# Convolution by interpolated products with two mixing stages: another order of the preparation, and attention maps with a pixel's blocks side by side

## The chip, the cores and the metric

The kernel runs on one core of a Trainium2 chip, as one program with one launch. The metric is the device time in microseconds of one execution. TensorE (PE) multiplies matrices into PSUM, ScalarE (ACT) and VectorE (DVE) read PSUM and work elementwise, GpSimd (POOL) does small things, and SyncE (SP) issues nearly all DMAs. Each engine takes its own instructions in order; they wait for each other through semaphores.

## The reference

The input is x, [4, 256, 48, 48] in float32. One layer is computed:

```
x = x + conv_attention(layer_norm_over_channels(x))
t = tokens(x);  t = t + ffn(layer_norm(t));  x = back(t)

conv_attention(x):
    k = relu(conv7x7(x, w1, dilation 2, padding 6) + b1)         # 256 -> 128 channels
    k = relu(batch_norm(w2 k + b2));  attn = softmax(k, 49 taps)
    out = sum over the 49 taps p of  x shifted by p  *  attn[:, p]
ffn: router on the mean token, two of 8 experts (256 -> 512 -> 256, gelu), weighted sum, layer norm
```

## The kernel before, in words

**Images.** With dilation 2, each of the four input images falls apart into four independent images of 24 x 24 pixels by the parity of row and column. These are the 16 images (`IMGS`) n = 0 to 15, four (`BI`) to each of the batches b = 0 to 3. A row strip `t` is 4 rows, 96 pixels, and an image has NT = 6 strips.

**Convolution.** Each row of the 7-tap kernel is done by evaluation at 14 points k (`NP`). The taps are transformed into `U`, the images into `V`, each split into a high and a low float16 part. Then `conv(b, k, c)` makes 21 matmuls (7 tap rows, three products of high and low parts) for channel half c, into one of three banks of `pM`. ScalarE (`copy_m`) and VectorE (`y_points`, L1009 to L1020) combine them into the 128 channels.

**Preparation.** Before the first product, `U` and the first four images of `V` must be there. The work is in four pairs of weight groups (`PAIRS_OG`), each pair with seven steps j (`U_PAIR`). `turn_u(u)`, u = 7 pair + j, is eight matmuls of a piece of weights with the table `Gs` (L1326). `turn_v(m)` is six matmuls with the table `Td` (L1311), and an image has six of them (`V_TURNS`). In the kernel before, `turn_v` m = 6 pair + j - 1 follows `turn_u` in the steps j = 1 to 6 of its pair: image n is turned in pair n. ScalarE writes the high halves (`u_high` L796, `v_high` L792), VectorE the low halves (`u_low` L965, `v_low` L961). TensorE may begin `turn_u(u)` when `u_low(u - 2)` is done, and `turn_v(m)` when `v_low(m - 2)` is done.

Between these, in the same in-order queues: for each pair, ScalarE sums the magnitudes of both weight groups (`magnitude(g)`, L784), VectorE puts them on a diagonal (`spread_mags`, L972), TensorE multiplies that (`bound`, L1333), VectorE makes the scale and the table `Gs` out of it (`tap_scale`, L979 to L995, whose last write is `back_w`), and the pair's first `turn_u` waits for that. For each image, VectorE takes the statistics (`ln_stats` L943, `ln` L952 to L956), GpSimd the inverse root (`rsqrt`, L719 to L725), ScalarE normalises in place (`normalise_x` L775) and writes the high half (`x_high` L840), VectorE the low half (`x_low` L1076), and `turn_v` waits for that. The order is written out by hand with constants that say in which step j each of them comes (`MAGS_THEN`, `NORM_PARTS`, `LN_PARTS`, `XHI_AT`, `SPREAD_AT`, `V_LATE`). On SyncE's queue the order of loads is: `ident`, weights 0 and 1, image 0, two tables, image 1, `w2` and small parameters, image 2, weights 2 to 5.

**Attention maps.** After a batch's logits and softmax, `turn_a(b, i)` (L1397) transposes the 49 taps of an image strip by strip into two banks, three strips of 96 pixels each. `a_high` (L833) and `a_low` (L1071) copy them as two float16 parts into a map of 49 rows and `MAP` = 600 columns: 576 pixels and 24 columns of padding. For batches 0 to 2 one instruction on each engine takes both banks. The maps of images 0 to 7 are stored to DRAM by DMA and loaded back in the last batch, those of 8 to 11 are written where they are read.

**Spreading.** An image is also cut into NB = 5 blocks of 5 rows (`TB` = 120 pixels; the last has 4 rows). `spread_taps(u)` (L1428) makes, for one pixel place in all blocks of all images of its group, one matmul whose moving operand is one column per image and block, out of the map `aT[g]`. In the map before, the blocks of a pixel lie `TB` columns apart. An item is 8 such matmuls (group 0: images 0 to 11, 60 or 48 columns) or 24 (group 1: images 12 to 15, 20 or 16 columns). Items go round three banks: item u waits until the low half of item u - 3 is taken (`spread_high` L869 on ScalarE, `spread_low` L1149 on VectorE). The 33 early items of group 0 are placed behind the convolution's halves of the last batch by `EARLY_SLOTS`: four behind (k = 9, c = 1), four behind each half at k 10 and 11, four and three at k 12, three and three at k 13. VectorE has `y_points` between the items of k 11 and of k 12 and searches maxima of expert weights (`take_unit`) up to k 10. After the last, `attend(n)` (L1444) multiplies the spread taps with the images, ScalarE evicts (`evict` L857), and the feed-forward part follows.

## Time and profile before

| | us |
|---|---|
| median of 3 runs | 963.73 (961.29 to 965.79) |
| the profiled execution, device time | 960.01 |
| its span, first to last instruction | 958.2 |
| TensorE busy | 904.5 (94%) |
| VectorE busy | 694.6 (72%) |
| ScalarE busy | 529.1 (55%) |
| GpSimd busy | 139.9 (15%) |
| mean granted TensorE clock | 0.975 |

The profile gives, for each engine, busy time and instruction counts, then the span in 40 slices, the chain of work that ended last, and groups of instructions with their mean duration and what ended the idle time before them.
### The profile page before, as it was taken

How to read it: one execution, taken by the hardware profiler on the slowest of the kernel's cores; microseconds unless marked ns; L12 is line 12 of the kernel's file. 1: busy time of each engine (PE TensorE's matmuls, PEld its weight loads, DVE VectorE, ACT ScalarE, POOL GpSimd, SP SyncE). 2: the span in 40 equal slices, each digit the busy share in tenths (PEclk: the TensorE clock that was granted, in tenths of full speed). 3: DMA queues.
4: the chain of work that ended last, by engine and by line, in shares of the span. 5: the costliest groups of instructions: out<-in, count | busy, mean ns of one | idle time of the engine just before them, and what ended most of it. 6: DMA issues, size and time to landing. Idle time of an engine off the chain costs nothing. (4 is left out here: it accounts for less than half of the span.)

```text
span 958.2 us, 19556 instructions
## 1 busy us (share of the span) xinstructions
PE 904.5 (94%) x7679; PEld 754.2 (79%) x7679; DVE 694.6 (72%) x1798; ACT 529.1 (55%) x981; POOL 139.9 (15%) x163
## 2 busy tenths in 40 slices
PE   2788999999999999999999959999999999999997
PEld 2777788888888888888999946777777777777776
DVE  3787467577658547865779858778877887788767
ACT  4796443543354321234445638768786878687751
POOL 1100100100001010200123211211212121212122
PEclk9799999999999999989999969999999999999999
DMA  9631132123210144540567563642465246323211
GB/s 222 185 95 50 50 80 70 52 57 98 58 34 26 41 137 143 175 79 2 149 181 216 149 176 78 153 104 53 98 151 101 50 100 165 84 69 82 67 34 50
DMA packets 134826, 95.01 MB, mean 99 GB/s; under 512 B 63579, under 2 KB 129516, under 8 KB 134636
## 3 DMA queue, kind: packets, MB, share of 16 engines
q1 hardware_dynamic: 134734, 93.77, 39.0%
q8 instruction: 60, 0.98, 0.4%
q14 instruction: 32, 0.26, 0.1%
HBM read 54.91 MB, written 29.40 MB: 88 GB/s over the span
## 5 line engine op out<-in xcount | busy, mean ns | idle before, releaser
L1340 PE MATMUL pM<-V,U 128*128 128x264 f16 (+3 forms) x2352 | 289.2, 280 | 2.2 <-DVE V L961 2.2
L1340 PEld LDWEIGHTS pM<-V,U 128*128 128x128 f16 x2352 | 227.8, 98 | 44.2 <-DVE U L965 2.4
L1876 ACT ACTIVATE gf<-pH,b1c,sc 128x384 f32<-128x384 f32 x192 | 127.6, 668 | 81.8 <-issue 67.2
L2166 PE MATMUL pH<-V,w1h 128*128 128x384 f16 x768 | 157.7, 328 | 1.8 <-ACT w1h L1848 1.8
L2180 PE MATMUL pY<-w2h,gh 128*128 128x256 f16 x576 | 157.0, 273 | 0.9 <-DVE w2l L2027 0.9
L2180 PE MATMUL pY<-w2l,gh 128*128 128x256 f16 x576 | 157.0, 273 | 0.0
L2180 PE MATMUL pY<-w2h,gl 128*128 128x256 f16 x576 | 157.0, 273 | 0.0
L2035 DVE SCALAR_TENSOR_TENSOR gl<-gf,sc,gh 128x384 f16<-128x384 f32 x192 | 112.0, 620 | 47.9 <-ACT gh L1867 47.9
L1867 ACT ACTIVATE gh<-gf,sc 128x384 f16<-128x384 f32 x192 | 115.4, 616 | 0.0
L2166 PEld LDWEIGHTS pH<-V,w1h 128*128 128x128 f16 x768 | 75.5, 98 | 50.0 <-issue 3.4
L792 ACT CAST V<-pV 128x336 f16<-128x336 f32 x96 | 41.8, 437 | 113.0 <-PE pV L1311 113.0
L2166 PE MATMUL pH<-V,w1l 128*128 128x384 f16 x384 | 94.5, 328 | 0.0
L961 DVE TENSOR_TENSOR V<-pV,V 128x336 f16<-128x336 f32 x96 | 47.1, 500 | 60.2 <-ACT V L792 60.2
L1815 POOL TENSOR_TENSOR tb<-V,bet 128x768 f32<-128x768 f32 x24 | 43.7, 1819 | 301.7 <-DVE z L2047 279.1
L1311 PE MATMUL pV<-Td,xs 96*128 96x168 f16 x576 | 58.4, 238 | 7.1 <-DVE xs L1076 6.2
L2180 PEld LDWEIGHTS pY<-w2h,gh 128*128 128x128 f16 x576 | 56.4, 98 | 8.9 <-issue 1.2
L2180 PEld LDWEIGHTS pY<-w2l,gh 128*128 128x128 f16 x576 | 56.4, 98 | 7.7
L775 ACT ACTIVATE xa<-xa,shift,rstd 96x256 f32<-96x256 f32 x96 | 49.7, 592 | 22.9 <-POOL shift L721 22.9
L2180 PEld LDWEIGHTS pY<-w2h,gl 128*128 128x128 f16 x576 | 56.4, 98 | 6.5
L719 POOL TENSOR_TENSOR rstd<-ve,mhalf 96x6 f32<-96x6 f32 x16 | 21.1, 1320 | 274.0 <-DVE nmean L956 274.0
L2166 PEld LDWEIGHTS pH<-V,w1l 128*128 128x128 f16 x384 | 37.6, 98 | 25.5 <-DVE w1l L1997 0.6
L1311 PEld LDWEIGHTS pV<-Td,xs 96*128 96x128 f16 x576 | 46.6, 99 | 12.1 <-issue 5.8
(251 smaller groups left out, 1351.9 us busy)
## 6 DMA issues: line engine op xcount, KB each, us to landing
xa<-in_xt SPq DMA_DIRECT2D x16, 576.0 KB, 6.5
xs_scratch<-xs SPq DMA_DIRECT2D x16, 576.0 KB, 4.3
V<-t_scratch SPq DMA_DIRECT2D x24, 384.0 KB, 3.7
out<-o SPq DMA_DIRECT2D x23, 384.0 KB, 2.9
xs<-in_ew SPq DMA_DIRECT2D x16, 512.0 KB, 4.3
U<-xs_scratch SPq DMA_DIRECT2D x16, 480.0 KB, 4.7
V<-in_w1g SPq DMA_DIRECT2D x6, 784.0 KB, 8.4
w1r<-in_ew SPq DMA_DIRECT2D x8, 512.0 KB, 4.4
```

The lines of the kernel that those rows point to most:

```text
L719: nc.gpsimd.tensor_tensor(rstd[:, n % 2], ve[:, n % 2], mhalf[:, :], ALU.pow).then_inc(rstd_step, 1)
L775: last = nc.scalar.activation(xa[:, n % XBUFS, t, :], xa[:, n % XBUFS, t, :], ACT.Identity, bias=shift[:, n % 2, t:t + 1], scale=rstd[:, n ...
L792: nc.scalar.copy(v_out(0, m), v_in(m)).then_inc(vhi_ready, 1)
L961: tt(v_out(1, m), v_in(m), v_out(0, m), ALU.subtract).then_inc(vlo_ready, 1)
L1311: last = nc.tensor.matmul(v_in(m)[:, :, r * TR * TILES:(r + 1) * TR * TILES], xs[:, n % 2, 2 * g + r, a, c * P:(c + 1) * P], Td[:, d, :], ...
L1340: return nc.tensor.matmul(out[:, :, first:end], U[:, k, hi_u, piece, :], V[:, b % 2, hi_v, k, c, :, first + TILES * d:end + TILES * d], st ...
L1815: nc.gpsimd.tensor_tensor(tb[:, s], tk[:, m % TBUFS], bet[:, None, :].broadcast_to([P, CT, C]), ALU.add).then_inc(bias_added, 1)
L1867: nc.scalar.activation(gh[:, s, j, :], gf[:, (JB * m + j) % GBUFS, :], ACT.Copy, scale=scale_of(G_UP)).then_inc(gh_ready, 1)
L1876: nc.scalar.activation(gf[:, (JB * m + j) % GBUFS, :], pH[:, (JB * n + j) % HBUFS, 0:CN], ACT.Gelu, bias=b1c[:, j // FB, j % FB:j % FB + 1 ...
L2035: stt(gl[:, sl, j, :], gf[:, (JB * m + j) % GBUFS, :], scale_of(G_UP), gh[:, sl, j, :], ALU.mult, ALU.subtract).then_inc(g_step, 1)
L2166: last = nc.tensor.matmul(pH[:, (JB * n + j) % HBUFS, 0:CN], w[:, k, c, f * P:(f + 1) * P], xT[:, s, x, c, :], start=(i == 0), stop=(i == ...
L2180: last = nc.tensor.matmul(pY[:, t, 0:C], g[:, s, j, t * P:(t + 1) * P], w[:, j // FB, j % FB, :], start=(i == 0), stop=(i == len(terms) - 1))
```

## The change

Part one changes the order of the preparation. `turn_v`, with its high and low halves, follows three steps behind the weights for images 0 to 2 (`V_LEAD` = 3: m = u - 3 for u = 3 to 20); image 3 stays in the steps j = 1 to 6 of pair 3. Weights 2 are loaded before image 1 and weights 3 after it. ScalarE takes the magnitude of group 2 before the loop and half of that of group 1; VectorE sums the other half (`add_half`). ScalarE does `u_high(0)` first, then normalises image 0, then `u_high(1)` and `x_high(0)`. The constants become pairs, one for pair 0 and one for the later pairs. In the later pairs `bound`, `spread_mags` and `tap_scale` come one step earlier than before. GpSimd's root for the batch norm comes after image 1's instead of image 2's.

Part two changes the maps of the first three batches: column `place * NB + block` instead of `block * TB + place`. The map is written in two pieces, strips 0 to 4 (480 columns, the four whole blocks) from the first bank and strip 5 (96 columns) from the second. `spread_taps` reads contiguous runs of `nb` columns for group 0. Group 1 is unchanged.

```diff
-    MAGS_THEN = (1, 3)
-    V_LATE = U_PAIR - V_TURNS
+    MAGS_THEN = ({3: 1}, {0: 0, 2: 1})
+    V_LEAD, V_LATE = 3, U_PAIR - V_TURNS
-    LN_PARTS, NORM_PARTS = {1: 0, 2: 1, 3: 2}, {0: 0, 2: 1, 4: 2}
-    XHI_AT, SPREAD_AT, BN_AT, LN_BACK_AT = 5, 4, 4, 5
+    LN_PARTS, NORM_PARTS = ({4: 0, 5: 1, 6: 2}, {1: 0, 2: 1, 3: 2}), ({4: (0, 1), 5: (2,)}, {1: (0,), 3: (1,), 4: (2,)})
+    XHI_AT, SPREAD_AT, BOUND_AT, SCALE_AT = (6, 5), (4, 3), (5, 4), (6, 5)
+    BN_AT, LN_BACK_AT = 5, 5
...
+        def turn_at(pair, j):
+
+            u = U_PAIR * pair + j
+            if pair < PAIRS_OG - 1:
+                return range(max(0, u - V_LEAD), max(0, u - V_LEAD + 1))
+            return range(V_TURNS * pair + j - V_LATE, V_TURNS * pair + j - V_LATE + 1) if j >= V_LATE else range(0)
...
+        def map_rows(flat, h):
+
+            rows = flat.rearrange("p (r w t) -> p t r w", r=BROWS, t=NB)
+            return rows[:, 0:NB - 1] if h == 0 else rows[:, NB - 1, 0:TL // SIDE]
+
+        def map_strips(n, h):
+
+            if n < EARLY:
+                return (range(NT - 1), range(NT - 1, NT))[h]
+            return range(h * NT // 2, (h + 1) * NT // 2)
...
+            load_w(sp, 2)
             load_x(1)
+            load_w(sp, 3)
...
-            for g in range(2, W_HOMES):
+            for g in range(4, W_HOMES):
                 load_w(sp, g)
...
-                    nc.gpsimd.memset(aTs[:, :, :, PIX:MAP], 0.0).then_inc(map_pads, 1)
+                    nc.gpsimd.memset(aTs[:, :, :, MAP - SIDE * NB + NB - 1:MAP:NB], 0.0).then_inc(map_pads, 1)
...
+                rows = KS * C // OG // (2 if g == 1 else 1)
...
-                parts, found = map_parts(b, i)
-                for h, (part, bank) in enumerate(found):
-                    act.wait_ge(aT_ready, 2 * n + (h + 1) * 2 // parts)
-                    nc.scalar.copy(map_to(n, 0, part, parts), bank).then_inc(ahi_ready, 2 // parts)
+                for h in range(2):
+                    act.wait_ge(aT_ready, 2 * n + h + 1)
+                    nc.scalar.copy(map_to(n, 0, h), map_from(n, h)).then_inc(ahi_ready, 1)
...
-            for g in range(2):
+            for g in range(3):
                 magnitude(g)
-            normalise_x(0)
...
-                    if pair + j == 0:
-                        x_high(0)
-                    if j >= V_LATE:
-                        v_high(V_TURNS * pair + j - V_LATE)
...
+                    if pair == 0 and j < 2:
+                        (x_high if j else normalise_x)(0)
+                    for m in turn_at(pair, j):
+                        v_high(m)
...
+            def add_half():
+                here, rest = mags[:, 1:2], mags[:, OGS:OGS + 1]
+                dve.wait_ge(w_loaded[1], 16)
+                nc.vector.tensor_reduce(rest, wst[1][:, KS * C // 2:], AX.X, ALU.add,
+                                        apply_absolute_value=True).then_inc(mag_added, 1)
+                dve.wait_ge(mag_added, 1)
+                dve.wait_ge(mag_ready, 2)
+                tt(here, here, rest, ALU.add).then_inc(mag_added, 1)
+                dve.wait_ge(mag_added, 2)
...
-                    first = block_0 * TB + h * SIDE + w % MO * TILES + w // MO
+                    place = h * SIDE + w % MO * TILES + w // MO
+                    where = (slice(place * NB + block_0, place * NB + block_0 + nb) if g == 0 else
+                             slice(block_0 * TB + place, (block_0 + nb - 1) * TB + place + 1, TB))
                     last = nc.tensor.matmul(spread_banks[u % SBANKS][:, o:o + imgs * nb], G[0:LO + TAPS, v, at:at + P],
-                                            aT[g][0:LO + TAPS, :, first:first + (nb - 1) * TB + 1:TB], start=True, stop=True)
+                                            aT[g][0:LO + TAPS, :, where], start=True, stop=True)
```

## Rows read from the trace of the kernel before

**Rows 1.** Stretches: us from:to, length, busy us (instructions) per engine, clock, DMA, GB/s.
```profile
0.00:20.00 20.00, 6.04 (x15) 4.97 (x16) 7.46 (x39) 5.94 (x8) 2.46 (x12) 1.00 0.97 216
...
140.00:300.00 160.00, 159.14 (x1523) 139.00 (x1522) 110.36 (x311) 69.91 (x137) 14.88 (x32) 1.00 0.23 60
...
422.91:430.55 7.64, 7.64 (x55) 6.41 (x54) 6.10 (x14) 2.23 (x4) 0.10 (x1) 0.73 0.00 0
```

**Rows 2.** Timeline, TensorE, preparation: start, us, instructions, [idle before <-releaser].
```profile
15.05 3.35 PE L1326 MATMUL pM<-work,V 112*128 112x224 f32 x8 [1.66 <-DVE back_w L995]
...
26.07 1.00 PE L1311 MATMUL pV<-Td,xs 96*128 96x168 f16 x6 [5.22 <-DVE xs L1076]
26.86 3.26 PE L1326 MATMUL pM<-work,V 112*128 112x224 f32 x8
...
43.20 2.54 PE L1326 MATMUL pA<-work,V 112*128 112x224 f32 x8 [2.08 <-DVE back_w L995]
...
96.31 9.83 PE L1340 MATMUL pM<-V,U 128*128 128x288 f16 x84 [2.19 <-DVE V L961]
```

**Rows 3.** Timeline, ScalarE, head of the preparation.
```profile
18.92 3.06 ACT L775 ACTIVATE xa<-xa,shift,rstd 96x256 f32<-96x256 f32 x6 [7.08 <-POOL shift L721]
...
22.67 1.47 ACT L840 CAST xs<-xa 96x1536 f16<-96x1536 f32 x1
...
27.44 1.70 ACT L784 ACTIVATE U<-V 112x1792 f32<-112x1792 f32 x1
```

**Rows 4.** Timeline, VectorE, head of the preparation.
```profile
17.03 2.05 DVE L943 BATCH_NORM_STATS2 st<-xa 96x6 f32<-96x256 f32 x6
...
22.80 1.09 DVE L965 TENSOR_TENSOR U<-pM,U 128x896 f16<-128x896 f32 x1 [2.90 <-ACT U L796]
```

**Rows 5.** DMA issues from 4.15 to 4.6 us: size, us from issue to landing (image 1).
```profile
xa<-in_xt SPq DMA_DIRECT2D x1, 576.0 KB, 11.7
```

**Rows 6.** One line's instructions: count, ns min/median/max, first to last start, form.
```profile
L833 ACT CAST xa<-pA x4: 632/632/632, 384.0 to 401.1; 49x576 f16<-49x576 f32 x4
...
L1071 DVE TENSOR_TENSOR xa<-pA,xa x4: 751/752/752, 384.8 to 401.9; 49x576 f16<-49x576 f32 x4
```

**Rows 7.** Timeline, TensorE, last batch and the stage after it.
```profile
400.34 0.66 PE L1397 MATMUL pA<-ident,E 96*66 96x96 f32 x6 [0.92 <-DVE xa L1071]
...
422.02 1.07 PE L1428 MATMUL pV<-xa,U 113*128 113x60 f16 x8
422.91 4.26 PE L1340 MATMUL pM<-V,U 128*128 128x288 f16 x21
...
427.88 1.07 PE L1428 MATMUL pL<-xa,U 113*128 113x60 f16 x8
428.77 1.97 PE L1428 MATMUL pV<-xa,U 113*128 113x60 f16 x16
430.55 3.86 PE L1340 MATMUL pM<-V,U 128*128 128x288 f16 x21
...
441.11 0.87 PE L1428 MATMUL pL<-xa,U 113*128 113x48 f16 x8
441.80 2.60 PE L1340 MATMUL pM<-V,U 128*128 128x288 f16 x21
...
452.14 0.51 PE L1444 MATMUL pM<-U,V 120*120 120x256 f16 x3 [1.21 <-issue]
...
513.51 0.90 PE L1428 MATMUL pL<-U 113*128 113x16 f16 x24
514.25 2.07 PE L1428 MATMUL pV<-U 113*128 113x20 f16 x48
```

**Rows 8.** Timeline, ScalarE, last batch.
```profile
421.34 0.56 ACT L869 CAST V<-pV 120x480 f16<-120x480 f32 x1 [0.33 <-PE pV L1428]
```

**Rows 9.** Timeline, VectorE, last batch.
```profile
421.93 0.66 DVE L1149 TENSOR_TENSOR V<-pV,V 120x480 f16<-120x480 f32 x1 [0.23 <-ACT V L869]
...
424.66 1.62 DVE L1015 SCALAR_TENSOR_TENSOR work<-pM,work 128x288 f32<-128x288 f32 x4
```

More of the change, by code:

```diff
@@ L547, in map_of, with map_to, map_from @@
             return aT[g][hl * LO:hl * LO + TAPS, n - GROUPS[g][0], :]
-        def map_parts(b, i):
-            if b < B - 1:
-                return 1, [(slice(0, PIX), pA[0:TAPS, :, 0:PIX // 2])]
-            return 2, [(slice(h * PIX // 2, (h + 1) * PIX // 2), a_bank(b, i, h)[0:TAPS, 0:PIX // 2]) for h in range(2)]
-        def map_to(n, hl, part, parts):
-            to = map_of(n, hl)[:, part]
-            return to.rearrange("p (h x) -> p h x", h=2) if parts == 1 else to
+        def map_rows(flat, h):
[5 more added lines that the diff above has]
+            return range(h * NT // 2, (h + 1) * NT // 2)
+        def map_to(n, hl, h):
+            if n < EARLY:
+                return map_rows(map_of(n, hl), h)
+            return map_of(n, hl)[:, h * PIX // 2:(h + 1) * PIX // 2]
+        def map_from(n, h):
+            bank = a_bank(n // BI, n % BI, h)[0:TAPS, 0:len(map_strips(n, h)) * TT]
+            if n < EARLY and h == 0:
+                return bank.rearrange("p (t r w) -> p t r w", t=NB - 1, w=SIDE)
+            return bank.rearrange("p (r w) -> p r w", w=SIDE) if n < EARLY else bank
         def sizes_of(b, numbers):
@@ L728, in _ @@
             rsqrt(1)
-            rsqrt(2)
             pool.wait_ge(bn_step, 1)
-            pool.wait_ge(size_step, 6)
+            pool.wait_ge(size_step, 4)
             nc.gpsimd.tensor_tensor(bnp[:, 6:7], bnp[:, 5:6], mhalf[0:TAPS, 0:1], ALU.pow).then_inc(bn_rstd, 1)
-            for n in range(3, IMGS):
+            for n in range(2, IMGS):
                 rsqrt(n)
@@ L783, in magnitude @@
                     act.wait_ge(mag_ready, g)
[L784 removed]
+                rows = KS * C // OG // (2 if g == 1 else 1)
+                nc.scalar.activation(spots[0:OG * KS, 0:rows, :], wst[g].rearrange("p (r n) -> p r n", n=OG)[:, 0:rows], ACT.Abs,
                                      accum_out=mags[:, g:g + 1]).then_inc(mag_ready, 1)
@@ L970, in spread_mags @@
                 for a in range(2):
+                    if pair == 0 and a == 1:
+                        add_half()
                     dve.wait_ge(mag_ready, 2 * pair + a + 1)
@@ L1067, in a_low @@
                 n = BI * b + i
-                parts, found = map_parts(b, i)
-                for h, (part, bank) in enumerate(found):
-                    dve.wait_ge(ahi_ready, 2 * n + (h + 1) * 2 // parts)
-                    tt(map_to(n, 1, part, parts), bank, map_to(n, 0, part, parts),
-                       ALU.subtract).then_inc(alo_ready, 2 // parts)
+                for h in range(2):
+                    dve.wait_ge(ahi_ready, 2 * n + h + 1)
+                    tt(map_to(n, 1, h), map_from(n, h), map_to(n, 0, h), ALU.subtract).then_inc(alo_ready, 1)
             def x_low(n):
@@ L1186, in _ @@
             for pair in range(PAIRS_OG):
+                late = min(pair, 1)
                 for j in range(U_PAIR):
-                    if j == U_PAIR - 1 and pair + 1 < PAIRS_OG:
+                    if j == SCALE_AT[late] and pair + 1 < PAIRS_OG:
                         tap_scale(pair + 1)
                     u_low(U_PAIR * pair + j)
-                    if pair + j == 0:
+                    if pair == 0 and j == 1:
                         x_low(0)
-                    if j >= V_LATE:
-                        v_low(V_TURNS * pair + j - V_LATE)
-                    if j in LN_PARTS and pair + 2 < BI:
-                        if LN_PARTS[j] < 2:
-                            ln_stats(pair + 2, third(LN_PARTS[j]))
+                    for m in turn_at(pair, j):
+                        v_low(m)
+                    if j in LN_PARTS[late] and pair + 2 < BI:
+                        if LN_PARTS[late][j] < 2:
+                            ln_stats(pair + 2, third(LN_PARTS[late][j]))
                         else:
                             ln(pair + 2, third(2))
-                    if j == SPREAD_AT and pair + 1 < PAIRS_OG:
+                    if j == SPREAD_AT[late] and pair + 1 < PAIRS_OG:
                         spread_mags(pair + 1)
@@ L1394, in turn_a @@
                 for h in range(2):
-                    for t in range(NT // 2):
-                        at = (h * NT // 2 + t) * TAPS
-                        last = nc.tensor.transpose(a_bank(b, i, h)[0:EPAD, t * TT:(t + 1) * TT],
+                    for slot, t in enumerate(map_strips(n, h)):
+                        at = t * TAPS
+                        last = nc.tensor.transpose(a_bank(b, i, h)[0:EPAD, slot * TT:(slot + 1) * TT],
                                                    E[:, i, at:at + EPAD], ident[0:TT, 0:TT])
@@ L1405, in _ @@
                     turn_u(U_PAIR * pair + j)
-                    if pair == 0 and j == V_LATE:
+                    if pair == 0 and j == V_LEAD:
                         pe.wait_ge(tab_loaded, 16)
-                    if j >= V_LATE:
-                        turn_v(V_TURNS * pair + j - V_LATE)
-                    if j == U_PAIR - 2 and pair + 1 < PAIRS_OG:
+                    for m in turn_at(pair, j):
+                        turn_v(m)
+                    if j == BOUND_AT[min(pair, 1)] and pair + 1 < PAIRS_OG:
                         bound(pair + 1)
```

16 lines of the change are left out of this document (9 added, 7 removed).

## The prediction

> **What bounds the kernel now.** I read three views in order: busy time by stretch, the timelines of TensorE, ScalarE and VectorE in the stages that the diff touches, and the waits there. The first [rows 1] says which resource matters: in the middle of the convolution (140 to 300 us) TensorE is busy 159.14 of 160 us, so work of other engines there is covered. The two stages that the diff touches are different. From 0 to 96.31 us the kernel prepares: the first convolution product starts at 96.31 [rows 2]. This is a lockstep of three engines: TensorE turns a piece of the taps (`turn_u`) or of an image (`turn_v`), ScalarE takes the high half out of PSUM, VectorE the low half, and two banks later TensorE may go on. From 403 to 452 us, in the last batch, the eight-matmul items of `spread_taps` stand between 21-matmul halves of the convolution; there TensorE never waits, so each us taken from it is worth a us until another engine takes over.
>
> **The head of the preparation.** Before, TensorE runs `turn_u(0)` at 15.05 and `turn_u(1)`, then stands 5.22 us for VectorE's low half of image 0 and starts `turn_v(0)` at 26.07, with `turn_u(2)` queued behind it at 26.86 [rows 2]. The chain behind that wait is on ScalarE: normalise image 0 (18.92, 3.06 us), the high half of `turn_u(0)`, high half of the image (22.67) [rows 3]; VectorE stands 2.90 us until 22.80 for the first of them [rows 4]. The change sends high half of `turn_u(0)` ahead of the normalisation, lets the images' turns trail by three steps, and does one magnitude of 1.70 us [rows 3] earlier, in ScalarE's idle time. It also takes half of the second magnitude to VectorE; that brings the first bound forward by perhaps 0.3 us, of which the image's first statistics, queued on VectorE, leave about 0.2.
>
> The new limit is a load. In SyncE's queue, weights 2 (784 KB) now precede image 1. Image 1 was issued at 4.2 and landed 11.7 us later [rows 5], at 15.9; 803 kB more at the 216 GB/s of the first stretch [rows 1] are 3.7 us, so it lands at about 19.4 (19.2 if the gap is that of one weight at a somewhat better rate). `ln(1)`, 2.05 us of statistics [rows 4] and some 0.8 of aggregation, stands ahead of the first `u_low` in VectorE's queue: 19.4 + 2.9 = 22.3, plus 1.1 for `u_low(0)` makes 23.4. So `turn_u(2)` starts at 23.4 instead of 26.86: 3.5 us gained.
>
> Then I laid the three queues out step by step, each instruction with its duration from the timelines and each wait from the code. Laid out for the kernel before this gives 96.0 for the start of the convolution, where the trace has 96.31. For the kernel after it gives pair 1's scale one step earlier, TensorE's wait for `back_w` before pair 1, 2.08 us ending at 43.20 [rows 2], cut to about 1.3, but three new waits of 0.5 to 0.8 us in pair 3 and one of 2.9 us for the magnitudes of pair 2 (they now stand behind image turns that pair 1 did not have). The convolution would start at 94.0: **2.3 us gained**. If image 1 landed at 21.5, the layout gives 96.2, no gain; if it landed at 16.9, 92.2. So 0 to 4 us. Moved DMAs: weights 2 and 3 land earlier, image 2, weights 4 and 5 later by up to 6 us, but image 2 is first read at about 33 and weights 4 at 41. The five parameter loads fall behind weights 3, to about 23; they are first needed at 28. GpSimd's square root for the batch norm goes ahead of image 2's: no one waits for it. What follows in the convolution is relative to its start.
>
> **The maps, written.** For the first three batches a map leaves PSUM in two pieces of 480 and 96 columns instead of one of 576 (0.632 us on ScalarE, 0.752 on VectorE) [rows 6]. The fixed part is paid twice: +0.2 us on each engine for each of twelve images. The writes are now ten bytes apart; no row shows such a write, so I bound it from nothing to the price of a far-apart column read below (1.8 ns where ScalarE now takes 1.1, 0.4 us more an image). I take nothing: up to the last batch it lies beside a TensorE that is busy throughout. Where it shows is one wait before the stage, 0.92 us ending at 400.34, in which TensorE waits for a map's low half [rows 7]: 0.2 us lost, at most 0.6. The pads are cleared with the same count of columns, and the stored and reloaded bytes are the same.
>
> **The maps, read.** This is where the time is. Eight matmuls of 60 columns are 0.89 us apart from the next item (422.02 to 422.91), 111 ns each; eight of 48 columns take 0.69 us (441.11 to 441.80), 86 ns [rows 7]. That is 1.8 ns a column, while a 288-column product of the same type takes 2.60 us for 21, 0.43 ns a column. The gap is the moving read: the columns of a block's pixels lie 240 bytes apart. Two rows say that it is a price of memory and not of the array: at 427.88 to 428.77 the item still takes 0.89 us though the products around it ran 4.26 and 3.86 us (the clock was at its 1.2 GHz level for part of that stretch, mean 0.73 [rows 1]), and the late group's 24 matmuls of 16 columns, also strided, take 0.74 us, 31 ns each [rows 7], in proportion to their columns. The last also bounds the weight load of 128 columns: below 31 ns.
>
> After, four or five blocks of a pixel lie side by side, and an item's matmul reads twelve runs of 4 or 5 neighbouring columns. Bounds: as cheap as the smallest seen, 31 ns for both; or as dear as before, 86 and 111. Between them: the first column of a run at 1.8 ns, the others at the product's 0.43, is 12 x (1.8 + 4 x 0.43) = 42 ns for 60 columns and 12 x (1.8 + 3 x 0.43) = 37 ns for 48. I take these, since it is the gap between columns that the rows show to be dear: 0.3 us an item of 48 and 0.34 of 60.
>
> The Trainium skill ("SBUF — State Buffer", section "Door 1: The DMA port swizzle") has the line behind this: SBUF has 16-byte cachelines and each access that crosses to a new one pays. The trace agrees as far as it can, with 1.8 ns a column at a stride of 240 bytes. A run of 10 bytes would cross such a line at four places in eight, one of 8 bytes at three, and the estimate by it is 50 and 43 ns. The skill also speaks against the change: by "TensorE: Matmul & The Clock Gate", section "LDWEIGHTS (loading the stationary operand)", 128 columns of weights take 128/1.2 = 107 ns, and then the contiguous maps would bring nothing. The late group's 31 ns speak against that here.
>
> But TensorE will then wait. Three banks hold the items; the fourth of a slot needs the first to have gone through ScalarE (0.56 us) [rows 8] and VectorE (0.66) [rows 9]. A slot of four 60-column items becomes 0.34 + 0.18 of drain + 0.56 + 0.66 + 0.1 of hand-over, then 0.34: 2.2 us instead of 3.5, and of 48 columns 1.95 instead of 2.75. A slot of three becomes 0.9 instead of 2.05. In order: slots at k 9 and 10, -0.8, -0.8, -1.4; k 11, -1.3 and then almost nothing, since VectorE is in the output points for 3.5 us (four of them are the row at 424.66 [rows 9]) and the items queue behind; k 12, -0.8, then -1.1; k 13, -1.1 and -1.1. Sum 8.4 us. The wait for the last low half, from which `attend` starts at 452.14 [rows 7], grows by 0.3. The two slow products, 1.66 and 1.26 over 2.60 [rows 7], make 2.9 us more if the clock does not fall; the stretch before the fall was the one richest in slow 60-column reads, which go. I take it as gained. Together 8.4 - 0.3 + 2.9 = **11.0**; with 31 ns for both the same sum gives 12.2, with 8 ns more than I take 10.4.
>
> **Sum.** 2.3 + 11.0 - 0.2 = 13.1 us. Against the profiled execution: span 958.2 to 945.1, its time 960.0 to 946.9. The median of the runs is 3.7 us above it, 963.7; from there **950.6**.
>
> **Rivals.**
> *The clock falls all the same* in two or three products of the stage. For: TensorE will stand 1 to 2 us in most slots, which it did not before. Price 2.9 us: 953.5.
> *The short runs don't help*, because a new run of five is as dear as a strided column, or the weights bind. For: no row shows a run that short. Against: 48 and 60 columns cost the same a column though their inner runs are 4 and 5. Only the head is left: 963.7 - 2.3 + 0.2 = 961.6, no difference that can be told.
> *The head gains nothing* because image 1 lands 2 us later than I think: 952.9.
> *Slower:* the waits between items hold the clock at 1.2 GHz from 403 us on. Its price is 1.66 us for each of the nine 21-product groups of the stage: 950.6 + 14.9 = 965.5. With the 2.9 us of before counted in, that is the whole gain of the stage and more, and each 10 us of matmuls that the level holds for behind the stage cost some 6 more (4.26 for 2.60 [rows 7]); it decides from about 5 us behind the stage, and with 20 us it gives 977. Against: the products still fill more than half of each slot.
> *More than I think:* reads at the floor and a head with image 1 at 17: 947 or less.
>
> **How the numbers follow.** A measurement of this kernel tells about 0.5% (4.8 us) from no change. Chances: the forecast 0.64, own range 947 to 955; clock 0.12; short runs 0.07; head 0.07; slower 0.05; more 0.05. The range takes the forecast, the clock case, the head case and most of the last: 945 to 957. Faster 0.88, same 0.07, slower 0.05.
>
> **What would show it.** Eight 60-column items' spacing between 0.26 and 0.4 us; new TensorE waits for VectorE's `alo_spread` of 1 to 2 us, largest at k 11; products all at 2.60; `attend` starting about 13 us earlier, at 439. In the head: `turn_u(2)` at 23 to 24, released by `u_low(0)` behind `ln(1)` and image 1's landing at 19.4; the convolution at 94. I am wrong in the maps if spacing stays over 0.6 us, and in the head if another wait than `ln(1)` stands before `u_low(0)`.

## The result, and the profile after

The kernel after takes 961.16 us in the median (951.57 to 963.22), beside 964.93 for the kernel before, 19 runs of each. The ratio is 0.9937 (0.9916 to 0.9959): 3.8 us faster, where I forecast 13.1. Its time lies above my range. Its profiled execution took 961.69 us, with a span of 959.9, and is longer than the one of before (960.01 and 958.2). The two profiles are therefore not two medians, and part of the work is to say why.

The page of after: busy time by engine, and the granted clock in 40 slices.

```profile
PE 898.7 (94%) x7679; PEld 746.1 (78%) x7679; DVE 706.1 (74%) x1812; ACT 540.8 (56%) x993; POOL 141.5 (15%) x163
...
PEclk9889999999999999989889959999999999999999
```

TensorE has 5.8 us less to do, although its clock is lower (0.967, before 0.975), and VectorE and ScalarE have 11.5 and 11.7 us more, where I had 0.2 us for each of twelve images, 2.4.

TensorE's timeline of after, in the preparation (start, duration, what it is, wait before it), answers to [rows 2]:

```profile
22.77 3.35 PE L1360 MATMUL pM<-work,V 112*128 112x224 f32 x8 [2.52 <-DVE U L988]
...
39.11 2.88 PE L1360 MATMUL pA<-work,V 112*128 112x224 f32 x8 [1.12 <-DVE back_w L1030]
...
54.14 1.11 PE L1367 MATMUL pM<-work,ones 112*128 112x224 f32 x2 [2.85 <-DVE work L1007]
55.05 3.19 PE L1360 MATMUL pM<-work,V 112*128 112x224 f32 x8
...
58.88 2.33 PE L1360 MATMUL pA<-work,V 112*128 112x224 f32 x8
...
96.16 9.83 PE L1374 MATMUL pM<-V,U 128*128 128x288 f16 x84 [2.19 <-DVE V L984]
```

The start of `turn_u(2)` moved from 26.86 to 22.77 and that of pair 1's first `turn_u`, which waits for `back_w`, from 43.20 to 39.11: 4.1 us ahead. Then TensorE stands 2.85 us before the `bound` of pair 2, and the first product starts at 96.16, which is 0.15 us ahead.

The same view in the last batch answers to [rows 7]. First the transposes and what waits, then the items of 48 and 60 columns, last `attend`:

```profile
394.81 0.66 PE L1431 MATMUL pA<-ident,E 96*66 96x96 f32 x6 [0.90 <-DVE xa L1105]
...
402.44 0.66 PE L1431 MATMUL pA<-ident,E 96*66 96x96 f32 x6 [2.13 <-DVE xa L1105]
...
406.74 0.68 PE L1464 MATMUL pV<-xa,U 113*128 113x48 f16 x16 [1.23 <-DVE xa L1105]
...
412.55 0.43 PE L1464 MATMUL pV<-xa,U 113*128 113x48 f16 x8
412.81 0.43 PE L1464 MATMUL pL<-xa,U 113*128 113x48 f16 x8
...
425.79 0.47 PE L1464 MATMUL pV<-xa,U 113*128 113x60 f16 x8
426.09 0.48 PE L1464 MATMUL pL<-xa,U 113*128 113x60 f16 x8
...
428.92 0.58 PE L1464 MATMUL pV<-xa,U 113*128 113x60 f16 x8 [2.04 <-DVE V L1182]
...
446.66 0.51 PE L1480 MATMUL pM<-U,V 120*120 120x256 f16 x3 [1.62 <-DVE U L1182]
```

Two things stand here. The items are as cheap as hoped: 412.55 to 412.81 is 0.26 us for eight matmuls of 48 columns, 32 ns each, and 425.79 to 426.09 is 0.30 for eight of 60, some 38 ns each. But before the first item there are waits of 0.90, 2.13 and 1.23 us for `a_low` (L1105), where before had one of 0.92. The lines of the map copies, with ns min/median/max, first to last start and forms, say why; they answer to [rows 6]:

```profile
L855 ACT CAST xa<-pA x8: 575/1051/1519, 383.7 to 404.3; 49x480 f16<-49x480 f32 x4, 49x96 f16<-49x96 f32 x4
...
L1105 DVE TENSOR_TENSOR xa<-pA,xa x8: 493/988/1495, 385.3 to 405.9; 49x480 f16<-49x480 f32 x4, 49x96 f16<-49x96 f32 x4
```

A map's pieces take 1.52 and 0.58 us on ScalarE and 1.50 and 0.49 on VectorE, where the whole map took 0.63 and 0.75.

The table follows the profile of each kernel that was run (us from the span's start). "Stage" is from the first matmul of `attend` to the last `turn_stats`; where matmuls were added ahead of `attend` (the three kernels with "late" in their name), both columns count from the first of the added ones, and their time at the full clock is taken off the stage. "Falls" is the number of stretches in the stage in which the clock goes to 1.2 GHz and comes back, each with some 3.4 us at the low level (one stretch of 6.8 us in maps_plain and one in order_ln count as two), without the one at the stage's end.

| kernel | median, all its runs | first product | first item | `attend` | stage | falls |
|---|---|---|---|---|---|---|
| before | 964.9 | 96.31 | 403.26 | 452.14 | 104.5 | 2 |
| after | 961.2 | 96.16 | 406.74 | 446.66 | 110.7 | 5 |
| after_again | 959.2 | 95.27 | 406.35 | 444.93 | 106.1 | 3 |
| after_third | 956.4 | 94.77 | 406.16 | 444.53 | 111.0 | 5 |
| maps_alone | 961.1 | 96.88 | 408.15 | 445.09 | 106.1 | 3 |
| order_alone | 971.0 | 96.62 | 404.21 | 454.75 | 112.4 | 6 |
| maps_plain | 954.0 | 96.31 | 403.57 | 442.09 | 109.4 | 5 |
| maps_runs | 953.5 | 95.98 | 403.53 | 442.15 | 106.1 | 3 |
| order_ln | 968.3 | 94.33 | 401.73 | 455.55 | 112.8 | 7 |
| after_runs | 955.4 | 95.44 | 403.46 | 441.93 | 109.9 | 5 |
| after_runs_ln | 947.2 | 93.13 | 400.54 | 437.48 | 106.2 | 3 |
| ln_again | 948.5 | 93.89 | 401.99 | 438.90 | 106.1 | 3 |
| before_late23 | 971.8 | 96.63 | 403.79 | 452.98 | 108.0 | 4 |
| before_late46 | 970.3 | 96.62 | 403.77 | 456.23 | 106.1 | 3 |
| ln_late23 | 954.7 | 94.23 | 402.23 | 439.14 | 109.4 | 4 |
| ln_late23_again | 953.1 | 93.97 | 401.79 | 438.71 | 109.4 | 5 |

The medians are over all executions, while the ratios below leave out five of order_ln's ten, those over 971 us, and one of after_again's ten, which took 5196.62 us and which no profile explains (the median of its other nine is 958.1).

Read the profile of after against that of before from left to right. At the first product 0.2 us is gained; from there to the first item 3.6 us are lost (310.58 for 306.95), from the first item to `attend` 9.0 gained (39.92 for 48.88), in the stage 6.2 lost, and behind it 1.0. Sum: 1.7 us lost, 959.9 for 958.2.

### The profile page after: what moved, and what is told of

The parts are those of the page before. It is cut to its first block and busy times, and to the rows that moved or that the text cites. A ratio compares the mean times of both kernels' runs of the same rounds, so it can differ in the third digit from the quotient of the medians.

```text
span 959.9 us, 19571 instructions
## 1 busy us (share of the span) xinstructions
PE 898.7 (94%) x7679; PEld 746.1 (78%) x7679; DVE 706.1 (74%) x1812; ACT 540.8 (56%) x993; POOL 141.5 (15%) x163
## 5 line engine op out<-in xcount | busy, mean ns | idle before, releaser
L2202 PE MATMUL pH<-V,w1l 128*128 128x384 f16 x384 | 94.8, 329 | 0.0
L1480 PE MATMUL pM<-U,V 120*120 120x256 f16 (+3 forms) x336 | 50.8, 286 | 3.7 <-DVE U L1182 1.6
```

Source lines behind the costliest of these rows:

```text
L1480: last = nc.tensor.matmul(pM[0:ko, (T_SUMS * n + u) % OBANKS, (t % 2) * C:(t % 2 + 1) * C], A[g][d, a][0:ki, n - GROUPS[g][0], t if d >= 0 ...
L2202: last = nc.tensor.matmul(pH[:, (JB * n + j) % HBUFS, 0:CN], w[:, k, c, f * P:(f + 1) * P], xT[:, s, x, c, :], start=(i == 0), stop=(i == ...
```

## The experiments

**First: each part alone, and the writes by themselves.** My theory then was that the gapped writes had cost what the reads gained, with the head as a smaller miss. maps_alone is the kernel before with part two of the change and nothing of part one; order_alone is the reverse:

```diff
 # maps_alone, against before
-                parts, found = map_parts(b, i)
-                for h, (part, bank) in enumerate(found):
+                for h in range(2):
...
+            rows = flat.rearrange("p (r w t) -> p t r w", r=BROWS, t=NB)
+            return rows[:, 0:NB - 1] if h == 0 else rows[:, NB - 1, 0:TL // SIDE]
...
+                                            aT[g][0:LO + TAPS, :, where], start=True, stop=True)
 # order_alone, against before
-    MAGS_THEN = (1, 3)
-    V_LATE = U_PAIR - V_TURNS
+    MAGS_THEN = ({3: 1}, {0: 0, 2: 1})
+    V_LEAD, V_LATE = 3, U_PAIR - V_TURNS
...
```

> Part two alone: the interleaved maps, with the preparation as before. Theory (writes and clock): the 480-column map writes take 1.5 us on ScalarE and VectorE as in the kernel after (0.63 and 0.75 us for 576 columns before), TensorE waits about 3 to 4 us more for a_low in the last batch, the stage of spread_taps is about 5 to 6 us shorter from its first product to attend, and what comes after depends on how often the clock falls in attend: 957 to 961 us in the runs. Rival (all of the change's gain is in the maps and the new preparation only costs): 2 us or more below the kernel after. Rival (as predicted before: 11 us gained): 953.

> Part one alone: the new order of the preparation, maps as before. Theory: the head gains 4 us up to turn_u(2) (22.8 against 26.9 us) and loses it again at the 2.85 us wait for the diagonal before pair 2 and in the slow clock behind it, so that the first product starts at 96 us as before: same time as before, within 1 us. Rival (the layout on paper): first product at 94.0, 2.3 us less. In both, the last batch and attend are as in the kernel before; if the falls of the clock in attend are a matter of the start time alone, they will differ in number from the kernel before although nothing there was changed.

maps_alone: 961.13, ratio 0.9952 (0.9921 to 0.9982). order_alone: 971.0, ratio 1.0044 (1.0007 to 1.0080). In the medians part two carries the gain, and part one alone is rather a loss. In their profiles the two parts do not lose in the same place: maps_alone has the 4 us before the first item (311.27 from the first product, before 306.95), order_alone has not (307.59), but has six falls in the stage and 112.4 us for 104.5.

maps_plain writes the two pieces contiguously, with the same number of columns and the new reads (held inside the map at its end); it leaves the interleaving out, so its values are wrong. maps_runs keeps every byte in its right place and turns the order of the write round: the block is the innermost dimension, so that four neighbouring columns are written as one run of 8 bytes, and PSUM is read with a stride of 120 columns instead.

```diff
 # maps_plain, against maps_alone
-                return map_rows(map_of(n, hl), h)
+                return map_of(n, hl)[:, (0, (NB - 1) * TB)[h]:((NB - 1) * TB, PIX)[h]]
...
 # maps_runs, against maps_alone
-            rows = flat.rearrange("p (r w t) -> p t r w", r=BROWS, t=NB)
-            return rows[:, 0:NB - 1] if h == 0 else rows[:, NB - 1, 0:TL // SIDE]
+            rows = flat.rearrange("p (x t) -> p x t", t=NB)
+            return rows[:, :, 0:NB - 1] if h == 0 else rows[:, 0:TL, NB - 1]
...
-                return bank.rearrange("p (t r w) -> p t r w", t=NB - 1, w=SIDE)
+                return bank.rearrange("p (t x) -> p x t", t=NB - 1)
```

> As maps_alone, but the map is written without a gap (strips side by side as before, 480 and 96 columns) and read in the new runs of 4 or 5; so pixels land at wrong places, the values of the spread taps are wrong, and the work and its sizes are the same. Theory (gapped writes cost): write of 480 columns 0.56 us on ScalarE and 0.66 us on VectorE, the waits for a_low at 395 to 407 us gone but for about 1 us, first item of spread_taps at 403.5 instead of 406.7 (as in the kernel after), attend at about 443: 3 to 4 us less than maps_alone. Rival (the waits come from the second instruction and not from the gaps): writes 0.56 us but at most 1 us less than maps_alone.

> As maps_alone with the same map, but the four whole blocks of a pixel are written one after another (8 bytes side by side, then a gap of 2) and PSUM is read with the stride instead. Theory A (each gap between written elements is dear, as with the reads): 480 columns in about 0.6 to 0.8 us instead of 1.5, and 2 to 3.5 us less than maps_alone. Theory B (PSUM read with a stride of 120 columns costs what the write saves): 1.5 us and no difference to maps_alone. Theory C (only whole runs without any gap are cheap): 1.2 us or more.

maps_plain: 954.04, ratio 0.9892 (0.9858 to 0.9925). maps_runs: 953.48, ratio 0.9890 (0.9846 to 0.9935). The lines of the map copies in the last batch, first of maps_plain, then of maps_runs:

```profile
L842 ACT CAST xa<-pA x8: 232/392/553, 383.9 to 401.8; 49x480 f16<-49x480 f32 x4, 49x96 f16<-49x96 f32 x4
...
L1079 DVE TENSOR_TENSOR xa<-pA,xa x8: 241/446/652, 384.5 to 402.5; 49x480 f16<-49x480 f32 x4, 49x96 f16<-49x96 f32 x4
```

```profile
L844 ACT CAST xa<-pA x8: 417/491/557, 383.6 to 401.7; 49x480 f16<-49x480 f32 x4, 49x96 f16<-49x96 f32 x4
...
L1081 DVE TENSOR_TENSOR xa<-pA,xa x8: 406/532/654, 384.2 to 402.4; 49x480 f16<-49x480 f32 x4, 49x96 f16<-49x96 f32 x4
```

480 columns cost 0.55 and 0.65 us when they are contiguous, the same when they go in runs of four with a strided read of PSUM, and 1.52 and 1.50 when each stands ten bytes from the next. The piece of 96 columns says the same within maps_runs: there it is still written at a step of ten bytes, and takes 0.42 and 0.41 us where maps_plain takes 0.23 and 0.24. (Why the same piece takes 0.58 and 0.49 in after stays open.) The first item comes 307.3 and 307.6 us behind the first product again, and `attend` at 442.1. The gapped write is shown as the cause of the loss before the first item, some 4 us in the profiles. The medians differ by 7, but maps_alone also ran at a lower clock (0.9705 for 0.9735 and 0.974 in the median); on the line of time against clock through each kernel's runs, it stands at 958.7 us at 0.972, the other two at 955.8 and 955.7, 3 us less.

**Second: the whole change with the new writes, and the head.** The 2.85 us before `bound` of pair 2 have a plain reason in VectorE's timeline of after:

```profile
52.16 0.74 DVE L966 BATCH_NORM_STATS2 st<-xa 96x6 f32<-96x256 f32 x2
...
53.63 0.46 DVE L1007 TENSOR_SCALAR work<-ident,mags 112x112 f32<-112x112 f32 x2
```

The last third of the statistics of the next image, with its aggregation (1.5 us from 52.16 to 53.63), stands in VectorE's queue ahead of `spread_mags`, for which TensorE waits. The edit brings the thirds one step earlier in the later pairs. after_runs is the whole change with the writes of maps_runs; after_runs_ln has the edit in addition; order_ln is part one alone with the edit; after_again is the kernel after once more.

```diff
 # after_runs_ln and order_ln
-    LN_PARTS, NORM_PARTS = ({4: 0, 5: 1, 6: 2}, {1: 0, 2: 1, 3: 2}), ({4: (0, 1), 5: (2,)}, {1: (0,), 3: (1,), 4: (2,)})
+    LN_PARTS, NORM_PARTS = ({4: 0, 5: 1, 6: 2}, {0: 0, 1: 1, 2: 2}), ({4: (0, 1), 5: (2,)}, {1: (0,), 3: (1,), 4: (2,)})
```

> The whole change, with the map written as in maps_runs (8 bytes side by side). If the preparation's new order is worth nothing in itself, this is as maps_runs, 953 to 954 us; if it loses its time by slower clock as order_alone did (6 us above the kernel before), it comes out at 956 to 960; if the preparation gains 2.3 us as first laid out, 951. First product at 96 us, first item of spread_taps at 403.5, attend at 442.

> As after_runs, and in the pairs behind the first the statistics of the next image come one step earlier on VectorE (steps 0, 1, 2 instead of 1, 2, 3), so that the 1.5 us of the last part no longer stand before the diagonal of the magnitudes. Theory: the wait before pair 2 goes from 2.85 to 1.6 us, the clock does not fall behind it (54 to 61 us at 1.00), the first product starts at 93 us. Rival: the clock falls there anyway and the start stays at 95 to 96. Total: 2 to 3 us below after_runs if the start of what follows is all that counts.

> The new order of the preparation alone, maps as before, with the statistics one step earlier as in after_runs_ln. Theory: first product at 93 us instead of 96.6; the last batch as before; the total is the kernel before less 3 us if the falls of the clock in attend do not depend on when attend starts, and anything from 956 to 970 if they do.

> The kernel after, unchanged, on the same chip as the others and with another profile. Expected 961 us as before. If the number of falls of the clock in attend is a matter of chance from run to run, the profile shows another pattern of them between 446 and 550 us than the first, and the runs' times go with the mean clock of each (0.967 at 961, 0.973 at 955).

after_runs: 955.39, ratio 0.9907 (0.9872 to 0.9943). after_runs_ln: 947.17, ratio 0.9835 (0.9816 to 0.9854), the fastest of all that computes the whole layer. order_ln: 968.34 (954.3 to 973.8), ratio 0.9947 (0.9905 to 0.9988). after_again: 959.17, ratio 0.9931 (0.9898 to 0.9965). TensorE's timeline of after_runs_ln:

```profile
53.51 0.65 PE L1367 MATMUL pM<-work,ones 112*128 112x224 f32 x2 [1.45 <-DVE work L1007]
...
93.13 7.08 PE L1374 MATMUL pM<-V,U 128*128 128x288 f16 x60 [2.19 <-DVE V L984]
```

The wait is 1.45 instead of 2.85, and the first product comes at 93.1 to 94.3 in the five profiles with this edit, against 94.8 to 96.2 in the three of the kernel after. So the head's forecast of 94.0 was within reach, one constant away. What does not fit in the medians is the sum: after_runs should have given both gains and is no faster than maps_runs.

**Third: the clock in the stage.** Over the runs of each kernel, time goes with the mean granted clock: the kernel before has runs of 960.5 us at 0.975, 964.2 at 0.972, 969.7 at 0.967 and 972.5 at 0.964, 10 to 11 us for each 0.01. The other kernels have about the same slope (8 to 13). The median clock is 0.972 for before and 0.968 for after. On that line, at 0.972, the parts add up: 964.1 for before, 962.1 for order_alone, 958.7 for maps_alone and 956.5 for after, so part one gives 2 us, part two 5.4 and both 7.6; and after_runs is at 953.4, 2.3 below maps_runs. Stretches of 10 us of after (length, busy us of the five engines, clock, DMA share, GB/s):

```profile
460.00:470.00 10.00, 10.00 (x83) 9.91 (x83) 4.72 (x21) 3.51 (x8) 1.87 (x4) 0.84 0.54 132
470.00:480.00 10.00, 10.00 (x81) 9.85 (x80) 7.75 (x31) 3.50 (x8) 1.37 (x2) 0.84 0.50 133
480.00:490.00 10.00, 10.00 (x66) 9.79 (x65) 4.63 (x18) 3.27 (x7) 1.37 (x2) 0.67 0.52 148
```

and the same three of before:

```profile
460.00:470.00 10.00, 10.00 (x97) 10.00 (x96) 7.71 (x32) 5.05 (x12) 1.59 (x3) 1.00 0.70 193
470.00:480.00 10.00, 10.00 (x83) 9.82 (x83) 6.42 (x25) 3.75 (x9) 1.37 (x2) 0.83 0.44 120
480.00:490.00 10.00, 10.00 (x97) 10.00 (x96) 6.90 (x32) 3.67 (x9) 2.30 (x3) 1.00 0.61 158
```

TensorE is busy in all of them, and yet does 66 to 83 matmuls in 10 us instead of 97 where the clock is below 1.00. The table's two last columns say what that costs: 104.5 us with two falls, 106.1 to 106.2 with three (six profiles of five kernels), 108.0 and 109.4 with four, 109.4 to 111.0 with five, 112.4 with six, 112.8 with seven. A fall costs some 1.7 us, half of its 3.4. The timeline of after shows what stands before one:

```profile
456.45 1.14 PE L1415 MATMUL pL<-w2T,work 128*96 128x49 f32 x12
457.43 2.52 PE L1499 MATMUL pA<-U,xs 120*128 120x1 f32 x20
459.81 0.87 PE L1480 MATMUL pM<-U,V 120*120 120x256 f16 x3
```

Twelve logit matmuls of 49 columns and twenty `sum_tokens` matmuls of one column, 3.4 us of small work, and behind them three `attend` matmuls take 0.66 us to the next start instead of 0.33. The stage has four such places with twenty `sum_tokens` matmuls in its first 50 us, and one near its end; the clock falls behind some of these and not behind others. Two theories were open: that it is chance, or that it depends on the time at which the stage starts, which every gained microsecond shifts. To shift the start alone, 2.5 or 5.0 us of matmuls of `attend`'s form were put ahead of `attend`, in the kernel before and in after_runs_ln:

```diff
 # 23 (before_late23, ln_late23) or 46 (before_late46)
+            pe.wait_ge(x_back[0], 32)
+            for _ in range(23):
+                nc.tensor.matmul(pM[0:TB, 0, 0:C], A[0][0, 0][0:TB, 0, 0, 0:TB], X[0][0:TB, 0, 0, :], start=True, stop=True)
```

> The kernel before with 23 more matmuls of attend's own form (256 columns, result overwritten) ahead of the first image of attend: 2.5 us of work at the full clock. If the falls of the clock in attend depend on when its images start, the time changes by something else than 2.5 us: the profile shows three to five falls (stretches of 10 us at 0.83) between 455 and 505 us as in order_alone, which starts attend 2.6 us late, and the runs come to 970. Rival (order_alone's falls have another cause): 965 + 2.5 = 967.5 and one fall.

> The same with 46 matmuls, 5.0 us. Phase theory: again another number of falls than with 23, in a range of 965 to 976 us. Rival: 970, in step with the work that was added.

> The fastest version (after_runs_ln, 947.2 us) with the 23 more matmuls ahead of attend. Phase theory: more falls between 445 and 505 us than its two, and 953 to 958 us. Rival: 947.2 + 2.5 = 949.7 with the same two falls.

before_late23: 971.76, before_late46: 970.32, with 969.38 for the kernel before beside them, on another chip than the runs so far (ratios 1.0039, 1.0008 to 1.0069, and 1.0029, 0.9992 to 1.0065). ln_late23: 954.72, ratio 0.9858 (0.9800 to 0.9915). Twice the added work gave no longer time in the medians, +0.9 for 5.0 us where +2.4 was measured for 2.5, and in the fast kernel 2.5 us of work made 7.6 us, though between two chips. The intervals of the first two hold the bare cost of the work, 2.5 and 5.0. At one clock, 0.972, on the line through each kernel's runs, the added work costs what it is: 966.5 and 969.1 against 964.1. So the start time may change the number of falls; but the number of falls is also not fixed for one kernel.

**Fourth: the pair that had differed most, side by side, and the cause of the falls.** few_sums keeps one of the five `sum_tokens` matmuls of each group:

```diff
 # few_sums, against after
-                    for t in range(NB):
+                    for t in range(1):
...
-                                                start=(t == 0), stop=(t == NB - 1))
+                                                start=(t == 0), stop=(t == 0))
```

> The kernel after, with sum_tokens cut from ten one-column matmul pairs to two per image, one block of the five (so the means of the tokens of two of the input images are wrong, and the router's numbers with them). That takes 1.9 us of these matmuls away behind each of the first four images and near the end. Theory: the clock falls in attend because logits (49 columns) and sum_tokens (one column) stand next to each other for 3.4 us; with 1.5 us of them left, it falls seldom, the mean clock goes from 0.968 to 0.975, and the time from 961 to 946: 8 us for the matmuls and 7 for the clock. Rival (the falls have nothing to do with these): 8 us alone, 953 at 0.968.

> The kernel after, for comparison on this chip: 957 to 962 us at a mean clock of 0.967 to 0.973.

> after_runs_ln again, beside its late version on one chip: 947 to 950 us at 0.977 to 0.979 if its good clock is its own; 950 to 957 if it was that chip's.

> after_runs_ln with 23 matmuls ahead of attend again. If the start time sets the falls: 4 us or more above ln_again, of which 2.5 are the work. If it was the chip: 2.5 us above it.

few_sums: 943.67, ratio 0.9774 (0.9708 to 0.9839). after_third: 956.41, ratio 0.9916 (0.9882 to 0.9950). ln_again: 948.45, ratio 0.9824 (0.9760 to 0.9888). ln_late23_again: 953.05, ratio 0.9868 (0.9803 to 0.9933).

In few_sums the clock does not fall once in the first 60 us of the stage, where the three profiles of the kernel after have four, two and four falls, and once in all of it. Its timeline at the place shown above, and a stretch of it behind:

```profile
455.59 1.14 PE L1415 MATMUL pL<-w2T,work 128*96 128x49 f32 x12
456.57 0.57 PE L1499 MATMUL pA<-U,xs 120*128 120x1 f32 x4
457.00 0.52 PE L1480 MATMUL pM<-U,V 120*120 120x256 f16 x3
```

```profile
460.00:470.00 10.00, 10.00 (x101) 10.00 (x99) 8.87 (x35) 5.48 (x13) 1.37 (x2) 1.00 0.69 194
```

The places of the falls can be compared between profiles, in us behind the first matmul of `attend` itself:

| profiles | clock falls at |
|---|---|
| after, after_third, after_runs | 12.8 to 12.9, 23.0 to 23.1, 33.3 to 33.4, 40.1 to 40.2, 77.7 |
| after_again, maps_alone, ln_again | 13.4 to 13.5, 23.6 to 23.7, 81.6 to 81.7 |
| maps_runs, after_runs_ln, before_late46 | 13.6, 30.7, 81.9 |
| before | 22.0, 80.0 |
| few_sums | 71.4 |

Different kernels have the same pattern, and the kernel after has two; the profiles that are not listed have others. The pattern goes with how the stage's start lies to the clock's falls ahead of it: in after, after_third and after_runs the last one begins 17.9 us before `attend`, in after_again 17.4, in maps_runs 17.1, and in few_sums 17.4. So after_again is the fair partner of few_sums, and it has the falls at 13.4 and 23.6 that few_sums has not. That the small matmuls behind the images are needed for the falls of the first 60 us is thereby well supported, by one profile of few_sums; every other profile has at least one such fall. The later falls seem to have another cause: few_sums has one too. The time of few_sums needs care: 96 matmuls are gone, at 0.11 us each (the 20 from 457.43 to 459.81 take 2.4) some 11 us, so of the 12.7 us to after_third only about 2 are more than work left out, though four falls fewer would be 6.8. Some of the rest went into waits at the stage's end: TensorE stands 2.4 us for GpSimd in front of the last `turn_stats`, 0.6 in after_again.

ln_late23_again is 4.6 us slower than ln_again for 2.5 us of work. Its profile has five falls, two more than ln_again's, all of the difference behind the first 60 us of the stage. All four of its runs are slower than all four of ln_again, by 2.9 us at the least. It leans to the start time, but four runs of each, with a scatter of 1 to 3 us, and the two late versions of before, whose intervals hold the bare cost of the work, do not settle it.

## Why the prediction was wrong, step by step

**The maps, read: right in mechanism, and in price within 16%.** I priced 48 and 60 columns at 37 and 42 ns; they took 32 and 38. TensorE waits for VectorE's low halves after that, 2.04 us at 428.92 as the largest, at k 11, as forecast. From the first item to `attend` I had 11.0 us; the kernel after gained 9.0, its repeats 10.3 and 10.5, maps_runs 10.3 and after_runs_ln 11.9. The term of 2.9 us for the clock was the wrong part of it: in after the clock is 0.91 over the 37 us from 403 to 440, as in before, so it falls there too. The gain goes with these falls: 9.0 us in after with two of them between the first item and `attend`, 10.3 and 10.5 in the repeats and 10.3 in maps_runs with one, 11.9 in maps_alone and after_runs_ln with none. The reads and waits alone, for which I had 8.4 - 0.3 = 8.1, gave 9.0. The two estimates from the Trainium skill in the prediction, 43 and 50 ns by lines crossed and 107 ns by the weight load, were too dear: 32 and 38 were measured.

**"The maps, written": the step that failed.** I wrote "I take nothing", with a bound of 0.4 us more an image and at most 0.6 us lost at one wait. The row nearest to a gapped write that I used was a gapped read by TensorE. The write measured 3.1 ns a column (1.5 us for 480) on both engines, 2.7 times the contiguous one on ScalarE and 2.3 times on VectorE. A map then takes 2.1 us on ScalarE, 1.5 more than before and not 0.4, and 2.0 on VectorE behind it, and TensorE stands for it three times in the last batch of after (0.90, 2.13 and 1.23 us). Cost: 3.6 us in the profile of after, 4.1 and 4.4 in its repeats. maps_plain and maps_runs, which differ from maps_alone by the writes alone, have none of it.

**The head: each wait as forecast, the sum not.** `turn_u(2)` at 22.77 (forecast 23.4), behind image 1's load and its statistics as forecast. These start at 18.85 in VectorE's timeline, released by that load; I had 19.4:

```profile
18.85 2.05 DVE L966 BATCH_NORM_STATS2 st<-xa 96x6 f32<-96x256 f32 x6 [1.93 <-DMA xa<-in_xt]
```

Then came the wait for `back_w` 1.12 (1.3), the wait before pair 2's `bound` 2.85 (2.9), three of 0.3 to 0.5 in pair 3 (0.5 to 0.8). But the product starts at 96.16, and in the repeats at 95.27 and 94.77, instead of 94.0. One missing term is the clock: in all six profiles with this wait (three of after, and order_alone, after_runs and few_sums) it falls to the low level between 53 and 57 us, and in the five with the statistics one step earlier it does not fall from 45 to 90 us. The stretch from the first turn behind it to 61 us, after:

```profile
55.05:61.05 6.00, 6.00 (x24) 5.29 (x23) 3.36 (x11) 2.65 (x3) 0.76 (x4) 0.58 0.00 0
```

At 0.58 of full speed the turn at 55.05 takes 3.0 us to the next start instead of 1.6, and the three turns of the stretch 6.0 us instead of 3.6 (1.56, 0.43 and 1.56 from 61.48 on): 2.4 us, about what the first product is late. My layout had no such stretch behind this wait. In after_runs_ln, where the wait is 1.45, the 10 us from 50 on have the clock at 1.00, in after at 0.66. The Trainium skill ("TensorE: Matmul & The Clock Gate", section "Part 1: The HAM clock gate") warns of just this, that idling throttles the engine and activity releases it. Here the trace agrees; in the stage behind `attend` it does not, since the clock falls there with TensorE busy for 10.00 of 10 us. And the wait itself was one constant away from being 1.45: I forecast it, and did not ask what stood ahead of `spread_mags`.

**Part one does not stand alone.** Its gain of 2 us at equal clock (962.1 for 964.1 at 0.972) is an estimate from the lines through the runs, but order_alone's runs have more falls than before's (6 for 2 in the profiles), and its median is 6 us slower. I had no rival for that. My rival "slower" had the clock at 1.2 GHz in the spread stage by waits; what happened was a stage further on, without a wait.

**The clock in the stage.** I counted the clock once, as 2.9 us in one place, and took before's profile as a state that the change leaves alone. It was among the fastest of before's runs: two falls, 960.0, where its median is 964.9. The kernel after has more falls in the median (clock 0.968 for 0.972), which is some 4 us at the slope above. The sum is then: head 0.2 to 1.5 instead of 2.3, writes 3.6 to 4.4 lost instead of 0.2, reads 9.0 to 10.5 instead of 11.0, clock some 4 lost instead of nothing; in the mean of the three profiles 0.9 - 4.0 + 9.9 - 4 = 2.8, beside 3.8 measured. This is rough, since the mean clock also holds falls ahead of `attend` that the first three terms count already.

Why after has more falls than before stays open. Those of the first 60 us need the small matmuls, as far as one profile of few_sums can show it. That their number depends on when the stage starts was tried with four kernels: the two from before do not tell it from the bare cost of the work, the two from after_runs_ln speak for it, not clearly. The Trainium skill ("TensorE: Matmul & The Clock Gate", section "Part 1: The HAM clock gate") says that the point at which the clock changes differs from run to run of one kernel, since its phase does not begin with the kernel. The three profiles of after, with 5, 3 and 5 falls, agree with that: the first fall comes 12.8, 13.4 and 12.8 us behind the start of `attend`, though the work up to it is the same. That this shift sets their number fits the table of places, but no run here changes it alone.

Against that doubt stands the result that needs no theory of it: after_runs_ln was the fastest whole kernel on two chips, 947.2 and 948.5, 1.7% below before, its clock 0.975 to 0.979. Most of its 8 us to after_runs (955.4, clock 0.970) goes with the clock; its late versions at 0.972, less their 2.5 us of work, stand at 952.4 and 952.0, some 1.2 below after_runs on its line (953.4), about the 1.4 us of the shorter wait.

## What to carry to other kernels

When a layout is changed for its reader, price the writer by a measured write of the same step, and put the shortest dimension innermost on the write: eight-byte runs with a strided PSUM read cost no more than contiguous ones here, single columns ten bytes apart 2.3 to 2.7 times as much. Before a forecast, look how the kernel's own runs scatter with the granted clock and where in that scatter the profile lies; compare kernels at equal clock, and treat falls as a number that the change may move. When a layout of queues shows a long wait of the critical engine, ask what stands ahead of its releaser: 1.4 us of it went by one constant.

## What the runs showed of the hardware

ScalarE and VectorE write float16 columns ten bytes apart at 3.1 ns a column, and contiguous or in runs of four at 1.1 to 1.4 (fixed part included). A PSUM read with a stride of 120 float32 columns costs them nothing (0.557 and 0.654 us for 480, against 0.553 and 0.652). TensorE reads runs of four or five neighbouring columns at 0.65 ns a column, weight load of 128 columns included. TensorE's clock falls behind 3.4 us of one- and 49-column float32 matmuls though the engine is never idle, in some executions and not in others, and mostly stays low for some 3.4 us; the falls stand at the same places in profiles of different kernels (12.8, 23.1, 33.3, 40.1 and 77.7 us behind the stage's start in three) and at others in a second profile of the same one (13.4, 23.6, 81.6). The same kernel scatters from 960 to 973 us with it.
